# Writing out the loop over pairs of sequences in a six-layer transformer on one Trainium2 core

## The reference, cut to what matters

```python
for i in range(DEPTH):                       # DEPTH = 6
    x = attn_layer(shift_tokens(x), Wqkv[i], q_scale[i], k_scale[i], Wo[i]) + x
    x = ffn_layer(shift_tokens(x), ln_g[i], ln_b[i], W1[i], b1[i], W2[i], b2[i]) + x

def attn_layer(x, Wqkv, qs, ksc, Wo):        # 16 heads of 64, window of 32 tokens
    q, k, v = split(x @ Wqkv)                # 128 -> 3 * 1024
    q, k = l2norm(q) * qs, l2norm(k) * ksc   # then turned (rotary)
    out = local_attention(q, k, v)           # each block of 32 sees itself and the one before
    return out @ Wo                          # 1024 -> 128
```

## Time and profile before

| what | value |
|---|---|
| median of three runs | 5327.94 us |
| the profiled execution | 5325.95 us |
| its span, first to last instruction | 5324.1 us |
| PE busy | 4457.0 us, 84% |
| PE weight loads busy | 3018.6 us, 57% |
| DVE busy | 3369.7 us, 63% |
| POOL busy | 2571.8 us, 48% |
| ACT busy | 2441.2 us, 46% |
| mean granted TensorE clock | 0.933 |

### The profile page before, as it was taken

The page is one execution under the profiler, slowest core; times in us unless marked ns, Lnnn a source line. Parts: engine busy times, 40 slices in busy tenths (PEclk is TensorE's granted clock), DMA queues, the critical chain, the costliest instruction groups (busy, mean ns, idle before and its releaser), DMA issues. The chain is left out here.

```text
span 5324.1 us, 183366 instructions
## 1 busy us (share of the span) xinstructions
PE 4457.0 (84%) x70226; PEld 3018.6 (57%) x70227; DVE 3369.7 (63%) x7024; ACT 2441.2 (46%) x5161; POOL 2571.8 (48%) x4541
## 2 busy tenths in 40 slices
PE   8999938676888888888888888888888888888885
PEld 5777725563555555555555555555555556555563
DVE  3555532475766567766677666766667666676765
ACT  4555543133554435554355544544435554354542
POOL 0000000004776547775376753767537776377761
PEclk9999959797999999999999999999999999999997
DMA  1000003101111101111011110111101111011110
GB/s 37 4 4 4 1 0 80 30 0 54 31 30 24 39 20 31 30 24 39 20 31 24 30 40 20 31 24 30 40 20 25 29 30 33 20 31 30 30 23 32
DMA packets 76046, 143.02 MB, mean 27 GB/s; under 512 B 19654, under 2 KB 57748, under 8 KB 68116
## 3 DMA queue, kind: packets, MB, share of 16 engines
q1 hardware_dynamic: 75284, 131.92, 10.3%
HBM read 35.40 MB, written 4.19 MB: 7 GB/s over the span
## 5 line engine op out<-in xcount | busy, mean ns | idle before, releaser
L2439 DVE TENSOR_TENSOR n_tt<-n_pp,n_rot 128x1024 f32<-128x1024 f32 x768 | 925.3, 1222 | 650.8 <-ACT n_sq L2309 647.8
L1941 POOL TENSOR_TENSOR n_pre<-n_tt 128x512 f32<-128x512 f32 x768 | 965.6, 1276 | 481.5 <-DVE n_tt L2439 480.8
L2057 PE MATMUL n_pp<-n_wqkv,n_xT 128*128 128x512 f32 x1536 | 828.6, 643 | 10.6 <-ACT n_xT L2304 10.5
L2309 ACT ACTIVATE n_sq<-n_pp 128x512 f32<-128x512 f32 x768 | 458.9, 598 | 797.2 <-PE n_pp L2057 793.4
L1976 POOL TENSOR_TENSOR n_pre<-n_pre,n_rn 128x512 f32<-128x512 f32 x768 | 777.6, 1045 | 36.8 <-POOL n_rn L1964 36.8
L2446 DVE TENSOR_REDUCE n_ss<-n_sq 128x8 f32<-128x512 f32 x768 | 519.5, 676 | 0.0
L2331 ACT ACTIVATE n_E<-n_E 128x512 f32<-128x512 f32 x384 | 235.8, 630 | 595.6 <-DVE n_E L2458 595.6
L2074 PE MATMUL n_pp<-ident,n_pre 128*128 128x128 f32 x3072 | 416.0, 278 | 45.4 <-POOL n_pre L1976 41.8
L2074 PEld LDWEIGHTS n_pp<-ident,n_pre 128*128 128x128 f32 x3072 | 361.3, 144 | 161.5 <-issue 94.4
L2320 ACT COPY n_qkT<-n_pp 128x512 f32<-128x512 f32 x768 | 420.7, 604 | 54.3 <-PE n_pp L2074 52.8
L2088 PE MATMUL n_pp<-n_wo,n_OT 128*128 128x128 f32 x3072 | 406.4, 287 | 4.9 <-ACT n_OT L2326 4.9
(11 more groups left out here) (263 smaller groups left out, 8241.4 us busy)
## 6 DMA issues: line engine op xcount, KB each, us to landing
n_Vx<-n_V SPq DMA_DIRECT2D x192, 256.0 KB, 3.8
n_Vx<-n_V SPq DMA_DIRECT2D x192, 192.0 KB, 3.7
n_wqkv<-in_L_ffn_Wqkv SPq DMA_DIRECT2D x6, 1536.0 KB, 7.4
e_w<-in_L_ffn_w SPq DMA_DIRECT2D x32, 256.0 KB, 3.0
m_Y<-e_ye SPq DMA_DIRECT2D x64, 64.0 KB, 2.0
n_wo<-in_L_ffn_Wo SPq DMA_DIRECT2D x6, 512.0 KB, 7.2
a_xs<-in_L_attn_x SPq DMA_DIRECT2D x16, 128.0 KB, 2.1
x_kept<-X SPq DMA_DIRECT2D x1, 2048.0 KB, 8.5
```

The costliest lines, as they stand in the source:

```text
L1941: nc.gpsimd.tensor_tensor(d, s[0], s[1][:, :, ::-1, :], ALU.add).then_inc(s_add, 1)
L2057: nc.tensor.matmul(pp[:, c % 2, :], xT[:, j * P:(j + 1) * P], wqkv[:, t * I + 512 * half:t * I + 512 * half + 512], start=True, stop=True) ...
L2309: nc.scalar.activation(sq[:, c % 2, :], pp[:, c % 2, :], ACT.Square).then_inc(s_sq, 1)
L2439: nc.vector.tensor_tensor(tt[:, c % 4, :, :].rearrange("p s (h d) -> p s h d", d=D), bcast(pp[:, c % 2, :].rearrange("p (h d) -> p h d", d ...
```

## The change

The middle loop is replaced by a Python loop, run when the program is built; all eight pairs of a layer are then straight code on PE, DVE, ACT and POOL. The loop over the layers and that of the feed-forward part stay, and so does SP's loop.

```diff
@@ -1858,10 +1858,8 @@
                 if layer_start:
                     layer_start(l)
                 prologue(l * NB, l)
-                pair(l, 0, True, False)
-                with eng.Fori(1, NB // 2 - 1) as i:
-                    pair(l, i, False, False)
-                pair(l, NB // 2 - 1, False, True)
+                for i in range(NB // 2):
+                    pair(l, i, i == 0, i == NB // 2 - 1)
                 feed_forward(l, l * NG)
```

## The result

| what | before | after |
|---|---|---|
| median of four runs | 5329.66 us (5325.83 to 5335.15) | 5139.43 us (5136.26 to 5145.20) |
| ratio | | 0.9644, 95% interval 0.9627 to 0.9660 |
| profiled execution | 5325.95 us | 5136.26 us |
| mean granted clock | 0.933 | 0.954 |

The changed kernel is 3.6% faster. The forecast was 5130 us in a range of 5095 to 5185 us; the median lies 9 us above the forecast.

What follows compares the result with a forecast made beforehand. PE was taken to bound the kernel, stalled by fetching code after 30 branches back. Sequences 2 to 13 were to fall from 2535.7 to 2340 us, so 5326 - 196 = 5130 us, range 5095 to 5185 us.

Steps and rivals of the forecast that it cites:

- What bounds the kernel: PE, busiest at 84%, idles 88.7 us before the masks at 30 branches back, fetching its code anew each pass.
- The gain by parts: On PE, 88.7 us of stalls plus 30 x 3.3 = 99 us of slow clock behind them, together 188 us.
- The straight sequence, 32.5 us: Sequences 2 to 13 as straight code: mean of four equally likely packet positions, 2340 us in place of 2535.7, gain 196 us.
- What was left out: Branch at the end of a layer and feed-forward loop: said to stay as they are, with no change in time counted.
- The other engines: DVE, ACT and POOL: lost branches gain nothing, about 120 new q14 packets counted at 0, 36 us kept in the range.
- What would show it: Signs: 30 stalls gone, sequences 2 to 13 about 390 us at clock 1.00, q14 up about 120, more `weigh` idleness under 1 us.
- Late code on the other engines: Each of 120 new packets on DVE, ACT and POOL costs 2.4 us that PE waits for: 5418 us; chance 0.04.
- Badly placed packets: Each of the twelve sequences has PE's bad packet position twice, 33.7 us a sequence: 5216 us; chance 0.06.
- the slow clock stays: PE's stalls go but its clock falls at some other idle moment: 5237 us; chance 0.04.
- all reading on is hidden: PE's straight code never waits at packet borders, 31.9 us a sequence: 5087 us; chance 0.06.
- nothing changes: The 2.9 us at the border between two pairs is not code fetching and stays in any form: 5326 us; chance 0.03.

Runs made afterwards that it cites:

- e1: Kernel before with only PE's loop over the pairs written out, DVE, ACT and POOL still looped; ratio 0.9643, 5129.45 us.
- e2: Kernel before with the pair loops of DVE, ACT and POOL written out and PE's loop kept; ratio 1.0009, 5323.85 us.
- e3: Kernel before with each middle pair written separately inside a one-pass loop, so branches are executed but never taken; ratio 0.9637, 5123.19 us.
- e8: Changed kernel with the loop over layers and the feed-forward loops written out too; ratio to the kernel before 0.9597, 5110.91 us.
- e6: Changed kernel with 64 more PE instructions once before the layers, shifting PE's code; ratio to the kernel before 0.9648, 5133.57 us.
- e5: Kernel before with a middle-loop body of two pairs and three passes, 12 branches back in place of 30; ratio 0.9780, 5203.92 us.
- e10: Kernel before, loops kept, PE's loop cut between scores and output projection, 24 jumps in place of 30; ratio 0.9869, 5250.99 us.
- e4: Kernel before, loops kept, PE's loop cut behind the projections of V, 24 jumps in place of 30; ratio 0.9837, 5230.59 us.
- e9: Kernel before, loops kept, PE's loop cut between output projection and output transposes, 24 jumps in place of 30; ratio 0.9712, 5168.06 us.

## Why the prediction was right

*What bounds the kernel.* Right: PE, stalled by its own jumps. e1 and e2 show the engine, e3 that the branch must be taken, and e8 and the moved edges that the price is that of the code behind it.

*The gain by parts, 89 us of stalls and 99 us of slow clock, 188 us.* The stalls went. The second term was taken from the length of one stretch, 3.3 us a jump, and holds more than the clock, but ends too early: the sums show 82 us of faster matmuls and 38 us of shorter waits, 120 us for what I had put at 99.

*The straight sequence, 32.5 us.* It measured 2326.45 / 72 = 32.31 us, so this term was too large by 0.2 us a sequence, 13 us in all. Taking a mean over positions was the right idea, as e6 shows, but the positions do not come one in four, and the one without idleness was put at 31.9 us, from sequence 14 and a correction. In the second layer four of the twelve sequences (4, 6, 8 and 12) have no idle moment and take 31.7 us; the other eight take 32.7 us in the mean, which is what the three positions with idleness had in the rows. Sequences 4 and 5 of the second layer, without an idle moment and with one of 0.93 us:

```profile
2049.61:2081.27 31.66, 29.34 (x648) 19.98 (x646) 24.71 (x37) 18.17 (x34) 24.95 (x46) 1.00 0.13 32
2081.27:2114.07 32.80, 29.55 (x648) 20.04 (x646) 24.89 (x37) 18.19 (x34) 25.33 (x46) 1.00 0.14 31
```

*What was left out.* I had said that the end of the layer and the feed-forward part stay as they are. The time outside the middle sequences grew by 19 us (16.5 us in the five borders, the rest in the last layer's end and in sequences 0 and 1). This step failed: work that is not changed does not keep its time when its code stands elsewhere and the engine in front of it is faster. Some 8 us are new waits for POOL in sequence 15, 6 us a longer stall at the start of a layer, and 3 us new idle moments in sequence 14. The two errors, 13 us of gain too little and 19 us of loss left out, nearly cancel, and that is luck: the profiled execution lies 6 us above the forecast, and the median 3 us above that.

*The other engines.* Right to count nothing for their code, within the 13 us that e2 leaves. But POOL did enter, as an engine that PE now waits for. Packets on q14 rose by 103 where 120 were worked out.

*What would show it.* The 30 entries are gone, and sequences 2 to 13 take 387 to 389 us at a clock of 1.00. I had expected more idle moments before `weigh`; there are fewer, 65 in place of 110. They stay under 1 us in sequences 2 to 13, reach 1.2 us in sequence 1 and 2.4 us in sequence 15. q8's packets, which were hardly to change, fell by 42 of 593.

*The rivals.* Late code on the other engines falls with e2. Badly placed packets, two late moments in one sequence, are not found in sequences 2 to 13; sequence 15 has them, where nothing long stands between `weigh` and the scores. That the slow clock stays falls with the clock of 1.00. That all reading on is hidden falls with 30.4 us still idle before `weigh` in sequences 2 to 13, which e6 moves about. That nothing changes falls with the result.

## What to carry to other kernels

When an engine's idle time before the first instruction of a loop's body is put down to nothing and occurs as often as the loop branches back, look at how much code the body has and whether it is fetched anew in each pass: PE's body was, with 12 packets a pass, while the bodies of the other engines were held and their branches were free. Write out the loop of that engine alone, or cut the loop where long instructions are queued in front of the edge and long ones follow it, which recovered 81% of the gain here, a fifth of the jumps having gone as well. Count the clock with the stall: a stall of 3 us cost 6. And look at what the engine runs into when it is faster: here it was POOL, for 8 us.

## What the runs showed of the hardware

- A jump on PE to code that is not held: 2.7 to 3.3 us of idleness with little queued (30 times in the kernel before, 12 in e5), and behind it a stretch at the lower clock, 0.50 in 2089.80:2095.80 of the kernel before; 6.0 to 6.3 us in all.
- A jump back on PE to code that is held (feed-forward loop): no packet on q8, no wait for "issue", and no gain from removing it (0.9597 against 0.9593).
- Where the loop is cut sets the price of its jump: 6.3 us, 5.0 (e10), 4.3 (e4) and 1.5 (e9). Behind the 24 stalls of 1.7 to 2.2 us in e9 the granted clock fell to 0.50 seven times; behind the 30 of 2.7 to 3.2 us in the kernel before, the 12 in e5 and the 24 of 3.5 to 4.9 us in e10 it fell each time.
- In e4 a second idle moment of 2.0 to 2.8 us follows, some 3 us behind the jump.
- Straight code is not free on PE: 0.3 to 1.2 us at an idle moment before `weigh` in sequences 1 to 14 of the changed kernel, and 1.4 to 2.4 us in sequence 15. On DVE, ACT and POOL 103 more packets cost at most 13 us together.
- Moving PE's code by 64 instructions moves these idle moments by one sequence, and the time of the kernel by 0.0004 of it, inside the interval.
